# Attention heads kept dimension-major: sums and shift turned by DMA and VectorE instead of by TensorE

## What is computed

```python
x = x + attn(layernorm(x))
x = x + moe(layernorm(x))

def attn(x):                       # H = 16 heads of hd = 16, S = 2048
    Q, K, V = (x @ W.T + b per head)
    A = softmax(Q @ K.T / sqrt(hd), axis=-1)
    L = local_diffusion_kernel(S)  # a normalised band of +-3 tokens
    out = (0.6 * A + 0.4 * L) @ V
    return out @ Wo.T + bo

def moe(x):
    p = softmax(gelu(x @ rW1 + rb1) @ rW2 + rb2)
    return sum over the 2 best e: p[e] * (gelu(x @ We1[e] + be1[e]) @ We2[e] + be2[e])
```

## Time and profile before

| what | value |
|---|---|
| median of 3 runs | 1991.12 us (1990.95 to 1991.9) |
| the profiled execution, first to last instruction | 2006.8 us |
| PE busy | 1951.3 us, 97% |
| DVE busy | 1626.5 us, 81% |
| ACT busy | 1374.2 us, 68% |
| POOL busy | 346.9 us, 17% |

### The profile page before, as it was taken

One profiled execution on the slowest core, in us unless ns is written; L12 is line 12 of the kernel. 1 busy time (PEld: TensorE's weight loads), 2 busy tenths in 40 slices (PEclk: granted clock), 3 DMA queues, 4 the chain that ended last, 5 costly groups with the idle time before them and its releaser, 6 DMA issues. The chain is left out here.

```text
span 2006.8 us, 47862 instructions
## 1 busy us (share of the span) xinstructions
PE 1951.3 (97%) x16384; PEld 1036.7 (52%) x16384; DVE 1626.5 (81%) x2075; ACT 1374.2 (68%) x2471; POOL 346.9 (17%) x379
## 2 busy tenths in 40 slices
PE   7999999999999999999999999999998799999997
PEld 3543333333333333333333333333687689999997
DVE  6799999999999999999999999994255565555564
ACT  3358888888888888888888888889544422233332
POOL 1361010001000100001000100010024532232233
PEclk9999999999999999999999999999999899999999
DMA  7954355335643454336534554341123677788884
GB/s 266 245 111 92 78 102 115 74 74 97 108 90 74 90 99 106 74 80 102 113 74 74 100 105 90 74 93 54 42 74 131 242 235 227 245 269 297 263 272 113
DMA packets 105849, 264.09 MB, mean 132 GB/s; under 512 B 20896, under 2 KB 52768, under 8 KB 99104
## 3 DMA queue, kind: packets, MB, share of 16 engines
q1 hardware_dynamic: 92624, 245.29, 48.6%
q0 software_dynamic: 13152, 17.83, 4.6%
HBM read 206.95 MB, written 73.94 MB: 140 GB/s over the span
## 5 line engine op out<-in xcount | busy, mean ns | idle before, releaser
L626 DVE TENSOR_REDUCE part_max<-psum 128x1 f32<-128x1024 f32 x1024 | 1240.8, 1222 | 50.6 <-PE psum L750 37.7
L681 ACT ACTIVATE probs<-psum 128x512 f32<-128x512 f32 x2048 | 1111.1, 596 | 145.4 <-PE psum L763 78.2
L763 PE MATMUL psum<-score_q,score_k 50*128 50x512 f32 x2048 | 745.9, 446 | 0.1
L750 PE MATMUL psum<-max_k,max_q 48*128 48x512 f32 x2048 | 737.9, 449 | 0.5 <-DVE part_max L626 0.4
L775 PE MATMUL psum<-probs,v_ones 128*32 128x256 f32 x8192 | 654.1, 391 | 9.4 <-ACT heads_sb L696 9.0
L763 PEld LDWEIGHTS psum<-score_q,score_k 50*128 50x128 f32 x2048 | 306.9, 184 | 404.7 <-ACT probs L681 390.7
L775 PEld LDWEIGHTS psum<-probs,v_ones 128*32 128x32 f32 x8192 | 162.1, 107 | 380.8 <-issue 198.1
L750 PEld LDWEIGHTS psum<-max_k,max_q 48*128 48x128 f32 x2048 | 294.2, 185 | 12.8 <-issue 7.0
L1184 ACT ACTIVATE x_sb<-psum,x_sb 128x512 f32<-128x512 f32 (+1 forms) x160 | 101.6, 636 | 257.8 <-PE psum L1564 243.1
L1583 PE MATMUL psum<-w,h_hi 128*128 128x256 f32 x1120 | 202.1, 279 | 2.7 <-DVE h_lo L1385 2.5
L1583 PEld LDWEIGHTS psum<-w,h_hi 128*128 128x128 f32 x1120 | 178.7, 189 | 13.8 <-DVE h_lo L1385 3.2
(11 more groups left out here) (185 smaller groups left out, 1352.3 us busy)
## 6 DMA issues: line engine op xcount, KB each, us to landing
w<-w_split SPq DMA_DIRECT2D x40, 2048.0 KB, 7.9
max_q<-qk_pieces SPq DMA_DIRECT2D x192, 128.0 KB, 7.2
score_k<-qk_pieces SPq DMA_DIRECT2D x192, 128.0 KB, 4.7
xs<-in_pads SPq DMA_DIRECT2D x33, 528.0 KB, 8.3
qk_pieces<-pieces SPq DMA_DIRECT2D x32, 512.0 KB, 4.6
w_split<-w_pair SPq DMA_DIRECT2D x32, 512.0 KB, 8.8
max_k<-qk_pieces SPq DMA_DIRECT2D x192, 64.0 KB, 8.2
score_q<-qk_pieces SPq DMA_DIRECT2D x192, 64.0 KB, 2.2
```

Source lines behind the costliest of these rows:

```text
L626: nc.vector.tensor_reduce(part_max[:, t, p:p + 1], ps_m[p].rearrange("q b f -> q (b f)"), axis=AXIS.X, op=ALU.max).then_inc(m_read, 1)
L681: nc.scalar.activation(probs[kb % 2][:, chunk * BLOCK:(chunk + 1) * BLOCK], bank_of(at), ACT.Exp, scale=float(HD) ** -0.5).then_inc(exp_do ...
L750: last = nc.tensor.matmul(ps_m[p][:, h, :], max_q[u][rows, t * P:(t + 1) * P], max_k[u][rows, p * BLOCK:(p + 1) * BLOCK], start=True, stop ...
L763: nc.tensor.matmul(bank_of(at), score_k[u][rows, kb * P:(kb + 1) * P], score_q[u][rows, part * BLOCK:(part + 1) * BLOCK], start=True, stop ...
```

## The change

PE makes no transposes in `attend` and no jump products any more, and the heads are never turned: they stay with the dimensions on partitions.

- *Normalising.* SP gathers the sums' rows of `heads_sb` to `sum_tok`, 128 partitions x 16 (`gather_sums`, 4 DMAs); DVE takes the reciprocal (`invert`, after key block 3's maxima); SP stores it to DRAM, waits for that, and loads it back over 16 partitions for each chunk (`spread_inverse`, 4 DMAs); POOL multiplies `heads_sb` by it in place; SP stores the head to the DRAM tensor `o` (4 DMAs). ACT's next copy to `heads_sb` waits for that store (`o_out`).
- *Shift.* DVE transposes `shift` in blocks of 32x32 to `shift_tok`, so that `load_shift` takes 16 DMAs of 8 pieces of 128 bytes.
- *Routing.* SP loads a block's heads to `o_block`, and DVE makes `attnT` as 0.6 times these plus the band's product in PSUM (`mix`), in place of ACT's copy.
- *Around them.* `probs` has 4 buffers instead of 2, `part_max` 2, the ring of PSUM banks has no extra units, and the loops run over six heads at a time (`by_head`). `xT_hi0` has a tile of its own.

```diff
-def twice(engine, pairs, body):
-    with engine.Fori(0, pairs - 1) as i:
-        body(i, False)
-    body(pairs - 1, True)
+def by_head(engine, body):
+    rounds = (NHEADS - 1) // SIX
+    with engine.Fori(0, rounds) as i:
+        for k in range(SIX):
+            body(SIX * i + k, SIX // 2 * i + k // 2, k, False)
+    for n in range(rounds * SIX, NHEADS):
+        body(n, n // 2, n - rounds * SIX, n == NHEADS - 1)
...
+def gather_sums(sp, keep, signal):
+    for c in range(BPS):
+        sp.dma_start(keep["sum_tok"][QUAD * c:QUAD * (c + 1), :],
+                     keep["heads_sb"][QUAD * c + HD:QUAD * c + HD + 1, :].rearrange("o (t q) -> o t q", q=ST)
+                     ).then_inc(signal, 16)
+def store_inverse(sp, dram, keep, signal):
+    sp.dma_start(dram["inv"].rearrange("(p t) -> p t", t=ST), keep["inv_tok"][:]).then_inc(signal, 16)
+def spread_inverse(sp, dram, keep, signal):
+    for c in range(BPS):
+        row = dram["inv"][c * BLOCK:(c + 1) * BLOCK].rearrange("(o f) -> o f", o=1)
+        sp.dma_start(keep["inv_rows"][QUAD * c:QUAD * c + HD, :], row.partition_broadcast(HD)).then_inc(signal, 16)
+def store_head(sp, dram, keep, place, signal):
+    for c in range(BPS):
+        sp.dma_start(dram["o"][ds(place, 1), :, c * BLOCK:(c + 1) * BLOCK].squeeze(0),
+                     keep["heads_sb"][QUAD * c:QUAD * c + HD, :]).then_inc(signal, 16)
...
         def load_shift(u):
-            for h in range(ROW_TILES):
+            for q in range(P // QUAD):
                 for c in range(PIECES):
-                    row, first = h * ROW_TILE + STACK + c, c * ST + h * ST // ROW_TILES
-                    sp.dma_start(score_q[u][row:row + 1, :].bitcast(F32).rearrange("o (t q) -> o t q", q=P),
-                                 shift_row[first:first + ST // ROW_TILES, :].bitcast(F32)).then_inc(shift_in[u], 16)
+                    for h in range(ROW_TILES):
+                        row, first = h * ROW_TILE + STACK + c, QUAD * q + c * ST + h * ST // ROW_TILES
+                        to = score_q[u][row:row + 1, :].bitcast(F32).rearrange("o (t q i) -> o t q i", q=P // QUAD, i=QUAD)
+                        sp.dma_start(to[:, :, q, :], shift_tok[first:first + ST // ROW_TILES, :]
+                                     ).then_inc(shift_in[u], 16)
...
+        def transpose_shift(m, loaded, loads):
+            dve.wait_ge(shift_ready, m + 1)
+            if loaded is not None:
+                dve.wait_ge(loaded, 16 * SHIFT_DMAS * loads)
+            nc.vector.transpose(shift_tok[:], shift[:].rearrange("p c t -> p (c t)").bitcast(F32)).then_inc(shift_tr, 1)
         def invert(n):
...
-            dve.wait_ge(exp_done, count_of(heads_unit(n)))
-            nc.vector.reciprocal(inv, tok[:, :, :, HD]).then_inc(inv_ready, 1)
+            dve.wait_ge(sums_in, 16 * BPS * (n + 1))
+            nc.vector.reciprocal(inv_tok[:], sum_tok[:]).then_inc(inv_ready, 1)
...
         def normalise(n):
...
+            pool.wait_ge(inv_in, 16 * BPS * (n + 1))
+            nc.gpsimd.tensor_tensor(heads_sb[:], heads_sb[:], inv_rows[:], ALU.mult).then_inc(scaled, 1)
...
         def copy_o(n):
+            act.wait_ge(o_out, 16 * BPS * (n + 1))
             act.wait_ge(pv_done, ST * (n + 1) + PV_OPEN)
             nc.scalar.activation(heads_sb[:], ps_o, ACT.Copy).then_inc(o_copied, 1)
...
+        def mix(i):
+            dve.wait_ge(heads_in[i % 2], 16 * KD * (i // 2 + 1))
+            for m in range(KD):
+                dve.wait_ge(a_ready[m], i + 1)
+                if m == 0 and i > 0:
+                    dve.wait_ge(o_ready, i)
+                nc.vector.scalar_tensor_tensor(attnT[:, m, :], keep["o_block"][i % 2][:, m, :], JUMP, ps_a[m],
+                                               ALU.mult, ALU.add).then_inc(a_copied[m], 1)
...
         for i in range(1, BLOCKS):
             load_band(i)
+            if i + 1 < BLOCKS:
+                sp.wait_ge(a_copied[KD - 1], i)
+                if i + 1 == HALF:
+                    sp.wait_ge(o_out, 16 * BPS * (NHEADS + 1))
+                load_heads(sp, dram, keep, i + 1, heads_in[(i + 1) % 2])
             store_residual(i - 1)
+            if i == 1:
+                sp.wait_ge(inv_ready, NHEADS + 1)
+                store_inverse(sp, dram, keep, inv_out)
+                sp.wait_ge(inv_out, 16 * (NHEADS + 1))
+                spread_inverse(sp, dram, keep, inv_in)
+                sp.wait_ge(scaled, NHEADS + 1)
+                store_head(sp, dram, keep, NHEADS, o_out)
```

More of the change, by code:

```diff
@@ L62 @@
 SHIFT_AT = 12
+INVERT_AT = 3
+PROBS = 4
+SIX = 6
 QUAD = 32
@@ L133, in load_score, with local_values @@
     load_stack(sp, dram, 1, K_ROWS, k_stack, n, False, signal)
[L136 removed]
+def local_values(nc, keep, out, i, m):
     b, kt = i // BPS, (i % BPS) * BT
[L139 to L141 removed]
+    band, v = keep["band"], keep["v"].rearrange("p b t h d -> p b t (h d)")[:, b, :, m * P:(m + 1) * P]
     for t in range(BT):
@@ L391, in attend @@
     v_ones = [sb(f"v_ones{u}", [P, ST, QUAD]) for u in range(2)]
[L392 to L396, removed]
+    probs, heads_sb, inv_rows, sum_tok, inv_tok = (
+        keep[n] for n in ("probs", "heads_sb", "inv_rows", "sum_tok", "inv_tok"))
+    part_max, neg_max, shift, shift_tok = (keep[n] for n in ("part_max", "neg_max", "shift", "shift_tok"))
     w_raw = sb("w_raw", [P, CHUNK])
@@ L408, in attend, with count_of, bank_of @@
     RING = 3
[L409 to L423, removed]
-        return at[0] + at[1] + 1
-    def bank_of(at):
-        return ps_s[at[1] % RING]
-    SHIFT_DMAS = PIECES * ROW_TILES
+    UNITS = CH * ST
+    def count_of(n, kb, c):
+        return n * UNITS + CH * kb + c + 1
+    def bank_of(k, kb, c):
+        return ps_s[(k * UNITS + CH * kb + c) % RING]
+    SHIFT_DMAS = PIECES * ROW_TILES * P // QUAD
     PARTS = 2
@@ L779, in values @@
                 last.then_inc(pv_done, 1)
-        def transpose_shift(out):
-            return nc.tensor.transpose(out, shift[:].rearrange("p c t -> p (c t)").bitcast(F32), ident[:])
-        def transpose_heads(out):
-            for c in range(BT):
-                last = nc.tensor.transpose(out[:, c * P:(c + 1) * P], heads_sb[:, c * P:(c + 1) * P], ident[:])
-            return last
         def project_v(r, t):
@@ L866, in _, with body @@
-        twice(pe, pairs, body)
+        def body(n, h, k, last):
+            u = k % 2
+            pe.wait_ge(v_in, n + 1)
+            for kb in range(ST):
+                ahead = kb + LOOK - ST
+                g, mu = ST * (n + 1) + ahead, (u + 1 + ahead // ST) % 2
+                more_maxima = not isinstance(n, int) or n + 1 + ahead // ST < NHEADS
+                more_scores = not (last and kb == ST - 1)
+                nxt = (n, k, kb + 1) if kb < ST - 1 else (n + 1, k + 1, 0)
+                if ahead == ST and more_maxima:
+                    pe.wait_ge(max_in[mu], 16 * STACK_DMAS * (h + 1 + u))
+                if kb == ST - 1 and more_scores:
+                    pe.wait_ge(score_in[1 - u], 16 * STACK_DMAS * (h + 1 + u))
+                    pe.wait_ge(shift_in[1 - u], 16 * SHIFT_DMAS * (h + 1 + u))
+                if more_scores:
+                    scores(*nxt, 0)
+                if more_maxima:
+                    maxima(g, ahead % ST, mu, 0)
+                if more_scores:
+                    scores(*nxt, 1)
+                values(n, kb, u, 0)
+                if more_scores:
+                    scores(*nxt, 2)
+                if more_maxima:
+                    maxima(g, ahead % ST, mu, 1)
+                if more_scores:
+                    scores(*nxt, 3)
+                values(n, kb, u, 1)
@@ L1131, in _ @@
     def _(act):
-        def copy_heads(i):
-            for m in range(KD):
-                act.wait_ge(a_ready[m], i + 1)
-                if m == 0 and i > 0:
-                    act.wait_ge(o_ready, i)
-                nc.scalar.activation(attnT[:, m, :], ps_a[m], ACT.Copy).then_inc(a_copied[m], 1)
         def copy_hi(i):
```

325 lines of the change are left out of this document (133 added, 192 removed).

## The result

The changed kernel takes 2581.05 us (median of 4 runs, 2564.88 to 2590.9), the kernel before 1991.19 beside it: a ratio of 1.295 (1.2915 to 1.299). It is slower, as forecast, but by 590 us and not by 376, outside the range that was given. The profiled execution has a span of 2586.2 against 2006.8, so 579.4 us are to be explained.

The account below looks back on a forecast made before the run. PE, DVE and ACT were taken as nearly equally full, with late shift loads and sums stretching heads to 52.4 us: 363 + 6.5 (start) + 7 (routing) - 1 (attention's end) = +376, giving 2367 us, range 2250 to 2450.

Parts of the forecast that it names:

- What bounds the kernel: PE, DVE and ACT within a few per cent of one another over a 40.69 us head; freeing PE alone brings little.
- rival 4: The 16 shift loads hide and DVE bounds a head at 40.1 us: 1979 us; chance 0.05.
- The shift: Sixteen shift loads at 0.68 us per issue on SP make PE wait 7.8 us in each head.
- The sums: DVE's reciprocal at key block 3 waits some 4.5 us a head for gathers queued behind SP's late loads.
- X + 18: Landing of the sums' gathers, 18 us after X, when the shift has landed and PE goes on; range 16.5 to 20.5.
- The clock: After idle time PE's clock stays low 3.4 us, losing 1.3 us; read from routing, counted in rival 1 only.
- rival 1: Gathers land before DVE wants them, so only the shift's wait remains; period 49.2 us, 2267 us; chance 0.17.
- the forecast's 11.7: Attention head period grows 11.7 us, from 40.69 to 52.4, adding 363 us over 31 heads.
- Routing: Constants wait 5, band wait 9, plus 1, less 8 for jump products: +7 us, between -8 and +20.
- its sign: DVE's reciprocal should wait for a DMA 3 to 6 us in most heads; without that wait, rival 1 holds.
- Rival 2: Shift loads issue at 0.46 instead of 0.68 us, 3.3 us less in each head: 2261 us; chance 0.12.
- Rival 3: Issue of 0.84, later gathers or fetching longer loop code costs 2 to 3 us more a head: 2440; chance 0.15.

Follow-up runs that it names:

- run 8: Changed kernel with 3 shift DMAs, transpose one key block earlier, reciprocal after key block 7, and two-head instead of six-head loops: 1992.16 us, ratio 1.000.
- run 1: Kernel before with only its 4 shift loads cut into 16, each of 8 pieces of 128 bytes: 2425.16 us, ratio 1.218.
- run 5: Changed kernel with the shift stored to DRAM and read back, 3 DMAs instead of 16, transpose one key block earlier: 2409.46 us, ratio 1.210.
- run 7: Kernel before with only its loop bodies holding six heads instead of two: 2025.66 us, ratio 1.017.
- run 2: Kernel before with 8 shift loads of 8 pieces of 256 bytes instead of 4 loads: 2264.27 and 2226.31 us.
- run 3: Changed kernel with 9 unread products on PE ahead of its wait for the shift: 2652.64 us, and one run of 10510.27.

## Why the prediction was right and wrong

**What bounds the kernel: right.** "Freeing PE alone can't bring much" is borne out by run 8: without the head's transposes and with both waits gone, a head takes 39.95 us instead of 40.69, as rival 4 had it (40.1). With its slow first two heads the whole of attention is 11 us shorter (1290.7 against 1301.9 from first scores to last copy).

**The shift: right to 0.1 us.** Sixteen issues in 10.80 us, by the rate of the four of before; 31 waits of 7.9 us, forecast 7.8; first scores at 130.9, as forecast. The shortest issue takes 620 ns, in both kernels, though the pieces are of 128 bytes here and of 512 there:

```profile
L493 SPq DMA_DIRECT2D score_q<-shift_tok x512: 620/626/1159, 118.6 to 1952.2; - x171
...
L654 DVE STREAM_TRANSPOSE shift_tok<-shift x32: 200/201/211, 118.4 to 1941.8; 128x32 f32<-128x32 f32 x32
```

The transpose is 0.20 us (0.25 was taken, an end at nothing and 0.5). The rule that the time to initiate a DMA "is usually small relative to the DMA itself" (the Trainium skill, DMA: Bandwidth & Descriptors, Issuing engines are not separate DMA queues) doesn't hold for transfers of 1 KB that are issued one behind the other: run 1 changes only their number and size, and loses 433 us of median time.

**The sums: right as a mechanism, and hidden by the other error.** In the changed kernel they cost 44.9 us instead of 31 x 4.5 = 140. Not because they land earlier: in run 5, where PE isn't late, DVE waits for them 30 times for 6.0 us. In the head shown above they land 18.1 us after PE goes on (809.2 less 791.1), and X + 18 was forecast. PE at the lower level simply arrives later, and the wait goes into that time.

**The clock: the step that failed.** The forecast took from the earlier trace rows that the clock is low for 3.4 us after a wait and that this costs 1.3 us. It put that into rival 1 and left it out of its own sum without giving a reason; the 4.5 us of waiting for the sums would have covered so short a slowdown. That was read from one place in routing. Measured, the lower level goes on for 4 to 43 us behind the first thirty waits for the shift, and for 802 us of work in all. Without the 58 us of the last head that is 24 us a head, and at 0.43 it costs 10.3 us instead of 1.3. The periods say nearly the same: 18.0 us more a head, less the forecast's 11.7 and 0.1, plus the 3.1 by which the waits for the sums shrank ((140 - 45) / 31), leave 9.3 for the clock. The slowdown of a product was taken nearly right: a pair took 1.22 for 0.74, 1.65 times, and a half step takes 2.16 for 1.23, 1.76 times. The duration was about seven times too short. The place it was read from explains how: in routing the upper level is back within 3 to 9 us of waits of 1.5 to 10.2 us in every kernel of this study, if it is left at all, and in attention mostly much later. Why the two stages differ no run shows.

**The last head** wasn't in the sum at all. It has no next shift to wait for, but the clock is low for 58 us, nearly all of it, behind the last wait (4.72 us), and it takes 19 us more.

**Routing: right.** The constants and the band came as forecast (the first `router` 41.3 us after the last copy begins, 25.0 in before and in runs 1 and 7: +16.3, forecast 14). From the third projection to the eighth PE then takes 78.6 us instead of 84.6 in runs 1, 2 and 7, so 6 us were gained, where 8 were counted for the jump products, less 1. The sum is +10 against these runs, forecast +7. The -6 against the span of before comes from that execution. The rows of the sum on DVE and of what PE waits for behind it:

```profile
2019.26 1.29 DVE L1308 SCALAR_TENSOR_TENSOR attnT<-o_block,psum 128x512 f32<-128x512 f32 x2 [57.07 <-DMA counting<-in_counting]
```

```profile
2020.70 5.91 PE L1471 MATMUL psum<-w_o,attnT 128*128 128x256 f32 x16 [6.09 <-DVE attnT L1308]
```

**The rivals.** Rival 1 (one wait only) didn't hold, though its sign is there: in most heads of the changed kernel DVE doesn't wait for the sums. Run 5 shows that the sign misleads. It was the one rival with a cost of the clock, but of 1.3 us. Rival 2 fell by the issue time. Rival 3 named the longer code, rightly as a cause, but it costs 34 us in all (1.1 a head) and not 2 to 3 us a head; its 2440 lies nearest to the measured time by luck, not by its mechanism. Rival 4's head time is real and its condition isn't: it needs the loads hidden, which run 8 does in another way.

**Still open.** Why the lower level lasts 9 us behind one wait and 22 behind the next, with the same work, and what brings the upper one back; why run 3 once took 10510 us; what the later reciprocal would bring the changed kernel by itself.

## What to carry to other kernels

Before cutting a transfer into more and smaller ones, count the issues on its queue between the moment the data is ready and the moment it is wanted. Price a wait on a full TensorE not by its length, but by its length plus the time at the lower clock behind it; here 2.0 us of wait cost 7.6 to 8.8 us of a head (235 and 273 us over 31 waits, run 2). And when one of two waits is taken away and the time doesn't move, take both away before giving up the theory.

## What the runs showed of the hardware

- In the attention loop each idle time of PE of 2.6 us or more was followed by the lower clock, and of the 31 of 2.0 us 22 were. It stayed for 4 to 58 us behind the wait, in run 2 with PE busy for 48 us of it, while in routing it was back in 3 to 9 us. A half step took 2.16 us against 1.23.
- A DMA with 8 pieces on one row takes SP 0.63 us to issue in the median, and 0.68 from start to start, for 128, 256 or 512 bytes a piece: the size doesn't enter, the number of DMAs does.
- Loop bodies of six heads instead of two brought PE gaps of 2.6 to 3.2 us at four ends of the loop, in either kernel, and 2.4 MB of instructions instead of 0.7.
- DVE's transpose of 128x32 in 32x32 squares takes 0.20 us, as long as a reduction of 128x32 (0.19).
